# An attention and feed-forward block on one core: the query projection after the weighing, its halves in two banks and by channel tile into the stack, and a reordered last batch

## What is computed

```python
r  = sigmoid(x) * num1 / max(den1, 1e-8) * (0.8 + 0.2 * tf)     # wkv1, from the side input k
q, k, v = split(r @ w_qkv.T + b_qkv)                            # 16 heads of 16
o  = softmax(q @ k.T / 4 + causal) @ v
x1 = x + o @ w_out.T + b_out
h  = sigmoid(x1) * num2 / max(den2, 1e-8) * (0.8 + 0.2 * tf)    # wkv2
y  = x1 + (silu(h @ ternary(W_up).T) * (h @ ternary(W_gate).T)) @ ternary(W_down).T
```

## Time and profile before

| | us |
|---|---|
| runs | 175.47, 175.5, 176.79 (median 175.5) |
| the profiled execution, its own time | 175.76 |
| its span in the profile | 173.9 |

### The profile page before, as it was taken

The page is one execution under the profiler, slowest core; times in us unless marked ns, Lnnn a source line. Parts: engine busy times, 40 slices in busy tenths (PEclk is TensorE's granted clock), DMA queues, the critical chain, the costliest instruction groups (busy, mean ns, idle before and its releaser), DMA issues.

```text
span 173.9 us, 3854 instructions
## 1 busy us (share of the span) xinstructions
PE 146.8 (84%) x1558; PEld 97.7 (56%) x1558; DVE 147.5 (85%) x255; ACT 115.5 (66%) x184; POOL 54.8 (32%) x57
## 2 busy tenths in 40 slices
PE   0007897977999799999999899999998999998992
PEld 0007882333378457754675567536855675787781
DVE  0599998999999999999958999994689999575673
ACT  2557976989877566598657354985572547886560
POOL 8800052999930086521000655310002232000000
PEclk9999999999999999999999999999999999999998
DMA  4899413505001323645630065347310000010001
GB/s 105 343 432 424 175 62 121 107 19 115 9 2 60 124 55 66 121 80 99 161 135 19 6 121 105 77 80 188 102 61 0 0 8 0 4 64 0 4 2 60
DMA packets 7290, 16.15 MB, mean 93 GB/s; under 512 B 936, under 2 KB 4456, under 8 KB 6888
## 3 DMA queue, kind: packets, MB, share of 16 engines
q1 hardware_dynamic: 5544, 10.52, 16.0%
q0 software_dynamic: 1440, 5.24, 15.3%
q10 hardware_dynamic: 288, 0.14, 0.4%
HBM read 6.43 MB, written 1.05 MB: 43 GB/s over the span
## 4 chain that ended last, share of the span: by engine, by line
PE 36%; DVE 23%; issue 6%; ACT 4%; POOL 2%; POOLq 1%; DVEq 0%; ACTq 0%
DVE row_max L711 7%; PE attn_ps L1144 7%; PE acc_ps L1068 4%; PE attn_ps L1039 3%; PE wide L1222 3%; PE wide L1117 2%; PE attn_ps L1234 2%; DVE hid L779 2%; PE wide L1122 2%; PE acc_ps L1004 2%; PE turn_ps L1004 2%; POOL hid_lo L296 2%; PE attn_ps L1186 2%; DVE x_hi L730 1%; PE turn_ps L1199 1%
## 5 line engine op out<-in xcount | busy, mean ns | idle before, releaser
L267 POOL TENSOR_TENSOR extra<-extra,k_t 128x512 f32<-128x512 f32 x7 | 10.0, 1426 | 62.4 <-DVE x_lo L736 43.4
L711 DVE TENSOR_REDUCE row_max<-wide 128x4 f32<-128x1024 f32 (+1 forms) x24 | 28.7, 1214 | 0.6 <-PE wide L1097 0.6
L428 ACT ACTIVATE probs<-wide 128x1024 f32<-128x1024 f32 x24 | 23.8, 1018 | 2.9 <-PE wide L1122 1.9
L466 ACT ACTIVATE silu<-attn_ps,up_scale 128x256 f32<-128x256 f32 x24 | 11.2, 473 | 21.4 <-PE attn_ps L1039 21.4
L624 DVE TENSOR_TENSOR_SCAN fwd<-decay,ek 128x256 f32<-128x256 f32 x32 | 23.1, 768 | 0.0
L636 DVE TENSOR_TENSOR_SCAN bwd<-ek,decay 128x255 f32<-128x255 f32 x32 | 20.2, 678 | 0.0
L1242 PE MATMUL wide<-ones 128*128 128x128 f32 x24 | 5.3, 421 | 14.0 <-DVE fwd L827 14.0
L296 POOL TENSOR_TENSOR hid_lo<-hid,hid_hi 128x512 f16<-128x512 f32 x9 | 11.1, 1239 | 15.0 <-ACT hid_hi L473 15.0
L1039 PE MATMUL attn_ps<-x_hi,w_tern 128*128 128x256 f16 x96 | 14.3, 274 | 1.1 <-DVE x_hi L730 1.0
L1039 PE MATMUL attn_ps<-x_lo,w_tern 128*128 128x256 f16 x96 | 13.9, 273 | 1.2 <-DVE x_lo L736 1.2
L1144 PE MATMUL attn_ps<-probs,v_pad 128*32 128x256 f32 (+1 forms) x192 | 12.6, 334 | 0.7 <-ACT probs L428 0.6
(11 more groups left out here) (156 smaller groups left out, 339.0 us busy)
## 6 DMA issues: line engine op xcount, KB each, us to landing
stack<-halves SPq DMA_DIRECT2D x24, 128.0 KB, 2.1
fwd<-extra POOLq DMA_DIRECT2D x5, 512.0 KB, 4.8
fwd<-bwd POOLq DMA_DIRECT2D x5, 512.0 KB, 4.4
w_raw<-wup_d SPq DMA_DIRECT2D x1, 1024.0 KB, 11.5
w_raw<-wgate_d SPq DMA_DIRECT2D x1, 1024.0 KB, 13.2
w_raw<-wdown_d SPq DMA_DIRECT2D x1, 1024.0 KB, 14.9
wqkv<-wqkv_d SPq DMA_DIRECT2D x1, 768.0 KB, 7.2
k_t<-k_d SPq DMA_DIRECT2D x1, 768.0 KB, 8.6
```

The source lines that it names most:

```text
L428: nc.scalar.activation(probs[:, j, :], flat(wide[j % 2][:, :, :]), ACT.Exp, scale=SOFTMAX_SCALE).then_inc(prob_done, 1)
L466: nc.scalar.activation(silu[:, e % 2], up, ACT.Silu, scale=up_scale[:, 0:1]).then_inc(silu_done, 1)
L711: nc.vector.tensor_reduce(out, src, AX.X, ALU.max).then_inc(max_done, 1)
```

## The change

Queries no longer fill `acc_ps`: channel tile 0 goes to `acc_ps`, tile 1 to the free half of `wide[0]`. ACT and DVE signal each tile of the q halves separately, and SP copies q by channel tile: four copies of 64 KB in place of three of 128 KB. The third part of q (the high half once more) is one copy of 128 KB, issued by POOL in batch 0 and by ACT in the others. In iterations 1 and 2 the query projection of the next batch follows the last `weigh`; it stood between pieces 3 and 4. Right behind it `project` now comes ahead of `values`. DVE's `refine`, `normalize` and `second_wkv` come ahead of the low halves of q, ACT's row reciprocals ahead of its high halves. In the last batch `tail_project(0)` comes ahead of the last `tail_score_t`, `tail_sigmoid` and the first reciprocal ahead of later exponentials, and `tail_project(1)` ahead of one `tail_up_gate` piece.

```diff
+        def wait_stacks(engine, n):
+            engine.wait_ge(second_in, 16)
+            engine.wait_ge(stack_in, 16 * (8 * n - 1))
+
+        def second_high(engine, b):
+            engine.wait_ge(zeros_q, 2)
+            engine.wait_ge(hi_done[0], CT * (b + 1))
+            if b >= 2:
+                engine.wait_ge(score_t_done, NT * (b - 1))
+            engine.dma_start(stacks[b % 2][2::4, 0, :, :], halves[:, 0, 0, :, :]).then_inc(stack_in if b else second_in, 16)
+
+        q_bank = (acc_ps[:, 0, :], wide[0][:, 0, 0:T])
...
+                for part, done in enumerate((hi_done[0], lo_done[0])):
+                    for ct in range(CT):
+                        sp.wait_ge(done, CT * b + ct + 1)
+                        sp.dma_start(stack[part::4, 0, ct::CT, :], halves[:, 0, part, ct, :]).then_inc(stack_in, 16)
...
             extra_products(1, 0)
-            pool.wait_ge(hi_done[0], 1)
+            second_high(pool, 0)
             values_of_keys(1)
...
+            def high_queries(b):
+                act.wait_ge(qk_done[0], b + 1)
+                if b:
+                    wait_stacks(act, b)
+                for ct in range(CT):
+                    nc.scalar.activation(halves[:, 0, 0, ct, :], q_bank[ct], ACT.Identity,
+                                         bias=vec[:, V_BQ + ct:V_BQ + ct + 1]).then_inc(hi_done[0], 1)
+                if b:
+                    second_high(act, b)
...
                     if b > 1:
-                        row_reciprocals(f)
                         extra_exp(1, b)
-                        copy_values(b)
                     nc.scalar.preload_act_table(ACT.Silu)
                     tanh_x1(f)
-                    if b == 1:
-                        copy_values(b)
+                    copy_values(b)
...
+                    if not more:
+                        first_reciprocal(1, b)
                     exp_probs(b, 4)
                     if more:
-                        high_halves(b + 1, 1)
+                        high_keys(b + 1)
                     else:
-                        first_reciprocal(1, b)
+                        tail_sigmoid()
                     exp_probs(b, 5)
                     if more:
                         first_reciprocal(1, b)
-                        high_halves(b + 1, 0)
+                        row_reciprocals(b)
+                        high_queries(b + 1)
...
-                    low_halves(b + 1, 0)
                     refine(1, b)
+                    normalize(b)
+                    second_wkv(b)
+                    low_queries(b + 1)
+                    if b + 2 < B:
+                        backward(0, b + 2, 0)
+                    else:
+                        backward(1, b + 1, 0)
...
+                if side == 0 and b:
+                    pe.wait_ge(prob_done, NT * (b - 1) + 5)
...
                     for j in range(2, NT):
+                        if j == NT - 1:
+                            tail_project(0)
                         tail_score_t(j)
                         if j < NT - 1:
                             tail_weigh(j - 2)
-                    tail_project(0)
...
                 weigh(b, 3)
-                queries_or_keys(b + 1, 0)
                 weigh(b, 4)
                 weigh(b, 5)
-
-            for part in range(2):
-                for e in range(2):
-                    tail_up_gate(e, (0,), part)
+                queries_or_keys(b + 1, 0)
+
+            for e in range(2):
+                tail_up_gate(e, (0,), 0)
+            tail_up_gate(0, (0,), 1)
             tail_project(1)
+            tail_up_gate(1, (0,), 1)
```

95 lines of the change are left out of this document (45 added, 50 removed).

## The result

The changed kernel took 176.53 us (median of 20 executions, 176.03 to 178.6), the kernel before 175.47 in the same comparison (20 executions, 175.43 to 176.81): 1.06 us more, a ratio of 1.0058 with a 95% interval of [1.0031, 1.0084]. That is less than the 1% which the prediction takes as the least that it can tell from no change, and it lies in the range of 174.0 to 176.9. But it is a loss and no draw: the interval leaves 1 out.

The account below looks back on a forecast made before the run. The prediction saw no engine alone as the bound, but a hand-over between them in every batch. Its terms, 0.47 + 0.1 - 0.74 + 0.2 = 0.03 us, gave 175.5 us, range 174.0 to 176.9.

Parts of the forecast that it names:

- batch 0: First batch: SP's extra q copy issue delays PE's scores on DVE's chain, +0.47 us, bounds -0.2 and +0.6.
- batch 1: Boundary 0 to 1: the last q copy lands later, half covered by DVE's work, +0.1 us, bounds 0 and +0.25.
- last batch: Sixth exponential behind the sigmoid makes the last `weigh` wait, +0.2 us, bounds 0 and +0.4.
- boundary 1 to 2: PE's wait for `x_lo` goes (-0.62), scores start late (+0.25): -0.37 us, bounds -0.62 and -0.24.
- boundary 2 to 3: Same stretch one iteration later, same claim: -0.37 us, bounds -0.62 and -0.24.
- One more issue stands ahead of the last landing: Batch 0, SP's queue: last issue at 27.38 instead of 26.78, PE starting at 29.43 instead of 28.96.
- The rival with GpSimd's copy: Batch 0: POOL's copy lands last, at 30.0, costing +1.1 us instead of +0.47; 176.1 us, chance 0.1.
- The cap of 0.62 us: Boundaries: PE's one wait for `x_lo`, 0.62 us, is the most that an earlier `x_lo` can give.
- the chain's 93.75: Boundary 1 to 2: time at which PE comes to the scores, 93.75 as now, 93.74 by the chain of waits.
- the row's 93.56: Boundary 1 to 2: the scores' start by the row's modelled start, 93.56, given beside the chain's 93.74.
- The 2.05: Boundaries: 2.05 us for the landing of the last 64 KB q copy, issued at 91.92; PE starts at 93.97.
- the last wants to start at 156.34: Last batch: the last of three `weigh` pieces, 0.91 us each, wants to start at 156.34 and waits until 156.6.

Follow-up runs that it names:

- e13: The kernel before with four filler products ahead of the transpose of the row maxima in batch 0; 175.42 us.
- e12: The changed kernel with four filler products ahead of the transpose of the row maxima in batch 0; 176.15 us.
- e3: The changed kernel with the last batch in the order of before, on ACT and on PE; 176.95 us, 175.90 at nearly full clock.
- e14: The kernel of e10 with four filler products ahead of the transpose of the row maxima in batch 0; 176.47 us.
- e1: The changed kernel with batch 0's q copies as before, three of 128 KB all issued by SP; 175.43 us.
- e2: The changed kernel with nine filler products instead of three on PE ahead of batch 0's first scores; 176.42 us.
- e5: The changed kernel with batch 0's third part of q issued by ScalarE instead of GpSimd; 176.58 us.
- e9: The kernel before with the new boundary order, ScalarE's third q copy in later batches and the new last batch, sixth exponential ahead of the sigmoid; 174.24 us.
- e11: The kernel of e9 with four filler products ahead of the transpose of the row maxima in batch 0; 174.24 us.
- e10: The kernel before with only the change's two banks, tile copies and their issuers, order and last batch as before; 177.61 us.

## Why the prediction was wrong

The forecast was a sum of four terms, 0.03 us in all, so no change. Their mechanisms are in the traces. What failed are the sizes of three terms, all to the slow side: batch 0, batch 1 and the last batch, together +1.43 us where the text has +0.77. The two boundaries gave what they were to give in four traces of six, but by two errors that cancel. And one thing, the clock, was not in the text at all.

| term | forecast | measured, e13 to e12 | in other traces |
|---|---|---|---|
| batch 0 | +0.47 | +0.75 | +0.73 (e3) |
| batch 1 | +0.1 | +0.27 | +0.27 (e14) |
| boundary 1 to 2 | -0.37 | -0.04 | -0.23 (profile after), -0.39 to -0.42 (e1, e2, e3, e5) |
| boundary 2 to 3 | -0.37 | -0.39 | -0.38 to -0.40 |
| last batch | +0.2 | +0.41 | +0.43 (profile after, from the first `weigh`) |

**Batch 0.** "One more issue stands ahead of the last landing" is right, and e5 shows that it is SP's fourth issue, not GpSimd's copy, that decides. The term is mis-sized: the first scores start 0.59 us later (28.65 in e13, 29.24 in e12), where the text has 0.47. One more issue puts the last one 0.66 later (26.46 and 27.12), since issues in a row lie 0.64 to 0.66 apart and not 0.60. The copy of 64 KB then lands 0.16 sooner than one of 128 KB, 1.98 against 2.14 us, and PE starts 0.14 after the landing instead of 0.05. The text had 0.13 for what the smaller copy saves up to PE's start (2.18 - 2.05); it was 0.07. The maxima start 0.71 later (29.62 and 30.33). The 0.12 between the two has a cause that the forecast ruled out by taking DVE to be idle there: with GpSimd's copy DVE's scans end 1.4 us later, which uses up the time that DVE had to spare and a tenth more (30.36 in the profile after, 30.25 in e5). The text did look at GpSimd's `values_of_keys(1)` being late, but only for who reads its result, and not for the scans that run beside it. About 0.05 more are there by the key projection of batch 1. The rival with GpSimd's copy had the right engine and the wrong mechanism, for the copy did not land last (27.69, SP's last 29.10). What the text cites of the Trainium skill ("DMA: Bandwidth & Descriptors", section on SWDGE, HWDGE and iDMA) is DVE that holds up GpSimd's descriptors. The runs show none of that: GpSimd's issue takes 0.76 us, shorter than its others (1.02 in the earlier trace rows), and its copy lands after 2.2 us. It was DVE that waited for GpSimd.

**Batch 1.** The bound of +0.25 was just passed. The last landing comes 0.50 us later against the key projection of batch 1 (9.03 and 9.53) and PE's scores 0.32, where the text has 0.23. Of this DVE's x2 work covered 0.05, where the text lets it cover half.

**The boundaries.** PE's wait for `x_lo` went, as forecast. Two steps failed, against each other. The cap of 0.62 us on the gain was too low: before, PE's products with `x_hi` (95.29) were paced too, 1.17 us of them up to the wait where the same eight take 0.88 now, so 0.91 us was to be had. And the scores start 0.50 us late against the key projection of batch 2 (12.00 us in e1, 11.50 before), where the text has 0.25. Of this 0.19 is the choice of the chain's 93.75 instead of the row's 93.56, and 0.05 the time from the start of SP's last issue to PE's start, 2.10 us and not 2.05. Net of both, 0.91 - 0.50 = 0.41: that the forecast of 0.37 is met is luck, since neither the gain nor the loss is as the text has it. The 2.05 was good in these four traces; in the profile after it is 2.29, which takes 0.19 from the boundary, and in e12 2.48. (The median landing over all sixteen copies of 64 KB is 2.0 us, 2.1 for those of 128 KB. The rule of the Trainium skill, "DMA: Bandwidth & Descriptors", section on the anatomy of one DMA, gives 2.15 and 2.3 as an estimate: both come out 0.15 to 0.2 too long here, but the step between them is right, since undisturbed copies take 1.98 and 2.14.)

**Last batch.** The sixth exponential was forecast to start at 155.6 and end at 156.6, and it did (156.92 and 157.93, less the offset of 1.38, are 155.54 and 156.55). The failed step is "the last wants to start at 156.34": that spread the three `weigh` pieces evenly over a stretch, and 154.45 + 2 x 0.91 is 156.27. The trace of before has the last one at 156.19, so its delay is 0.40 and not 0.26.

**The clock.** The text did not speak of it. TensorE's granted clock was full throughout the profiled execution of before (0.996 in the mean), and one of its three times shown, 176.79, was 1.3 us above the others; that was a sign that some executions differ by something. The whole difference of the medians is 1.06 us, that of e12 and e13 0.73. The remaining third is what is left for half-clock stretches, long and short, in the executions of the changed kernel. That is what remains, and not a measured part; its lowest, 176.03, is 0.6 above the lowest of before. Whether the long ones are more frequent in it (8 of 20) than before (45 of 126) is not shown. Without the clock the sum of the terms as measured gives +0.63 (+1.0 in the pair of e12 and e13) where +0.03 was forecast.

**What the chances were worth.** Of the rivals none came as such. The measured time lies 1.0 us above the 175.5 forecast, outside the 0.6 us around it that had a chance of 0.5. Three terms came out above their upper bounds at the same time (+0.6, +0.25 and +0.4), and two of them share one cause: an issue of half the bytes takes the queue as long, and its landing saves only 0.16 us of the 0.65.

**A version that beats both** is the one of e9 with the filler of e11: the new order at the boundaries, the copies in 128 KB with the third issued by ScalarE, the last batch with its exponential ahead of the sigmoid. It takes 174.24 us in the median, 174.01 to 174.32 in six executions. The ratio of 0.9892 flatters it, because 10 of the 19 executions of before beside it had the long stretch. Against the kernel before with the same filler (e13, 175.42) it is 1.18 us, 0.7%, and its trace puts 1.17 of this at the boundaries (0.17 and 1.00) and 0.10 in the last batch. The filler itself changes no time at full clock; it keeps the slow executions away.

## What to carry to other kernels

Cutting a copy in two doubles its time in the issuing queue. Before a tile is copied in pieces to start sooner, count the issues ahead of the last landing: here four steps of 0.65 us replaced three, the smaller copy landed 0.16 us sooner, and the piece that arrives last decides. When an issue is given to an engine that also computes, ask what it pushes back there, and what runs beside that. Where several small terms share one unknown price, their bounds don't cancel: the range of the sum has to move them together. And when a few executions in the list lie apart from the rest, look at the granted clock by stretches before adding tenths: with a wait of PE of 1.2 us a third of the executions lost 1.2 us elsewhere, and with four filler products in that wait none of 42 did in this way. The same part can also differ between two traces of one program (0.4 us at boundary 1 to 2), so a term read from one pair of traces needs a second pair.

## What the runs showed of the hardware that was not expected

- A scan of 128x256 in float32 on DVE takes 0.66 us alone. One that starts 0.4 to 0.8 us into a TENSOR_TENSOR of GpSimd takes 1.07 or 1.58 us and ends 0.55 us after GpSimd's, in every trace here. In every trace in which GpSimd first issues a copy of 128 KB (the changed kernel, e2, e3, e10, e12, e14) the first of batch 0's scans takes 2.43 to 2.45 us and ends 0.56 after GpSimd's product behind that issue. With ScalarE or SyncE as the issuer it takes 1.08 (e5, e1).
- SyncE's issue of 64 KB into 32 strided partitions takes 0.60 us in the median, as one of 128 KB, and the next in a row starts 0.64 to 0.66 after it. It lands after 2.0 us in the median (1.9 to 2.5), against 2.1 (2.1 to 3.1).
- An issue by ScalarE takes 0.54 to 0.61 us of its queue, and the engine's next instruction started 0.71 to 0.80 us after the end of the one before the issue.
- Of executions of the same program on the same chip some run for about 7 us at 1.2 GHz and others don't. PE had waited 1.22 us before the stretch in the trace of the changed kernel. With that wait filled with products no execution had a long stretch (0 of 42); with products removed 10 us earlier they were frequent (9 of 12).
